# A graph-attention kernel: three late adjacency halves packed and loaded during the plan, two late tiles searched ahead of the first unit

## The reference

```python
h = jnp.maximum(_layernorm(x), 0.0)
hh = jnp.einsum('ni,hif->hnf', h, W)
s1 = jnp.einsum('hnf,hf->hn', hh, a1)
s2 = jnp.einsum('hnf,hf->hn', hh, a2)
scores = leaky_relu(s1[:, :, None] + s2[:, None, :], 0.2)
scores = where(adj[None] > 0, scores, -9e15)
att = softmax(scores, axis=-1)
o = jnp.einsum('hnm,hmf->hnf', att, hh)      # heads side by side: (6144, 512)
return x + elu(o)
```

## Time and profile before

| | us |
|---|---|
| three runs of the kernel before | 792.19, 793.66, 800.2 |
| median | 793.66 |
| the profiled execution | 800.12 |
| its span, from the first to the last instruction | 798.2 |
| VectorE busy in it | 659.8 (83%) |
| TensorE matmuls busy in it | 570.5 (71%) |
| ScalarE, GpSimd busy in it | 469.2, 424.6 |
| granted TensorE clock, mean | 0.848 of full speed |

### The profile page before, as it was taken

One profiled execution on the slowest core, in us unless ns is written; L12 is line 12 of the kernel. 1 busy time (PEld: TensorE's weight loads), 2 busy tenths in 40 slices (PEclk: granted clock), 3 DMA queues, 4 the chain that ended last, 5 costly groups with the idle time before them and its releaser, 6 DMA issues.

```text
span 798.2 us, 9153 instructions
## 1 busy us (share of the span) xinstructions
PE 570.5 (71%) x2182; PEld 407.3 (51%) x2182; DVE 659.8 (83%) x2066; ACT 469.2 (59%) x695; POOL 424.6 (53%) x804
## 2 busy tenths in 40 slices
PE   0389789898877777653777677677767669988770
PEld 0255445554444444342566465556655558766560
DVE  4659988999886767764879998999979989999871
ACT  0777797799999989324265655666455123333231
POOL 4634444443442432227666466647675776888720
PEclk9989999999998989855879879686887769997895
DMA  9999988899999999418989999999998888999986
GB/s 287 423 365 384 349 330 341 338 378 420 419 422 419 419 419 424 196 40 312 389 325 410 414 402 387 406 395 410 392 405 282 216 239 231 284 279 277 285 236 160
DMA packets 65130, 269.51 MB, mean 338 GB/s; under 512 B 12145, under 2 KB 12145, under 8 KB 52786
## 3 DMA queue, kind: packets, MB, share of 16 engines
q1 hardware_dynamic: 32098, 177.95, 55.5%
q0 software_dynamic: 26368, 78.36, 32.3%
q10 hardware_dynamic: 6608, 12.58, 4.2%
HBM read 243.49 MB, written 25.37 MB: 337 GB/s over the span
## 4 chain that ended last, share of the span: by engine, by line
DVE 20%; PE 16%; issue 10%; ACT 3%; another core or an unknown queue 3%; DMA 1%; POOL 1%; POOLq 0%; DVEq 0%; ACTq 0%
DVE nodes L1122 7%; PE psP L1260 5%; PE psP L1261 4%; DVE places L250 3%; PE psP L1267 3%; PE psP L1268 3%; DVE best L239 2%; ACT packed L229 2%; PE psC L1244 2%; DMA nodes<-table,list_column 1%; DVE agg L1134 1%; POOL nodes L959 1%; DVE to_row L1092 1%; DVE result L1142 1%
## 5 line engine op out<-in xcount | busy, mean ns | idle before, releaser
L651 PE MATMUL psH<-sb_W,normedT 128*128 128x512 f32 x384 | 222.5, 671 | 0.0
L229 ACT ACTIVATE packed<-adj_rows,eight 128x3072 uint8<-128x3072 int32 x66 | 188.5, 2856 | 3.8 <-DMA adj_rows<-in_adj_dram 3.2
L954 POOL DMA_INDIRECT nodes<-table,column x138 | 138.5, 1003 | 68.4 <-issue 39.5
L1260 PE MATMUL psP<-nodes,ident 128*128 128x256 f32 x276 | 107.8, 480 | 53.0 <-issue 40.1
L959 POOL DMA_INDIRECT nodes<-table,list_column x109 | 110.8, 1017 | 64.2 <-DVE list_column L1081 33.6
L1122 DVE TENSOR_TENSOR nodes<-nodes,psW 128x2048 f32<-128x2048 f32 (+4 forms) x66 | 138.7, 2142 | 5.1 <-ACT psW L1029 5.0
L698 POOL TENSOR_TENSOR sb_node_sum<-sb_node_sum,h_rows 128x512 f32<-128x512 f32 x48 | 61.1, 1273 | 141.4 <-ACT h_rows L616 141.4
L652 PEld LDWEIGHTS psS<-sb_Wa,normedT 128*128 128x128 f32 x384 | 78.1, 203 | 101.8 <-issue 101.8
L250 DVE FIND_INDEX8 places<-best,packed 128x8 uint32<-128x96 f32 (+6 forms) x240 | 110.4, 468 | 0.0
L239 DVE MAX8 best<-packed 128x8 f32<-128x96 f32 (+6 forms) x240 | 103.2, 463 | 4.5 <-ACT packed L229 4.5
L1261 PE MATMUL psP<-nodes,ident 128*128 128x264 f32 x276 | 104.5, 467 | 0.0
(11 more groups left out here) (177 smaller groups left out, 925.0 us busy)
## 6 DMA issues: line engine op xcount, KB each, us to landing
adj_rows<-in_adj_dram SPq DMA_DIRECT2D x66, 1536.0 KB
sb_adj_rows<-in_adj_dram SPq DMA_DIRECT2D x30, 1536.0 KB, 12.7
table<-h_rows SPq DMA_DIRECT2D x48, 260.0 KB, 8.7
sb_x_rows<-in_x_dram SPq DMA_DIRECT2D x48, 256.0 KB, 8.9
result<-in_x_dram POOLq DMA_DIRECT2D x19, 512.0 KB
out_dram<-result ACTq DMA_DIRECT2D x19, 512.0 KB
result<-in_x_dram POOLq DMA_DIRECT2D x10, 256.0 KB
out_dram<-result ACTq DMA_DIRECT2D x10, 256.0 KB
```

The lines of the kernel that those rows point to most:

```text
L229: nc.scalar.activation(words.bitcast(mybir.dt.uint8), sb["adj_rows"][buffer_of(i)][:], ACT.Square, bias=sb["eight"][:], scale=-17.0, accum ...
L651: nc.tensor.matmul(psH[:, t % 2], normedT[:, t % 2, kc], sb["W"][:, kc], start=(kc == 0), stop=(kc == KC - 1))
L954: nc.gpsimd.indirect_dma_start(out=nodes[:, node_at[u] + i * w.direct + j], out_offset=None, in_=table, in_offset=bass.IndirectOffsetOnAxi ...
L1260: nc.tensor.matmul(low, sb["ident"][:], nodes[:, n, 0:LOW], start=a, stop=False)
```

## The change

The late halves 60, 61 and 62 (both halves of tile 30 and the first of tile 31) are packed by ScalarE in the plan, and the halves 63, 64 and 65 are issued by SyncE in the plan, each behind one of these packs and all ahead of the store of `mean_row` in SyncE's program. In the edges, VectorE searches tiles 30 and 31 ahead of unit 0, in two pieces: the first three MAX8 of tile 30 between `own(1)` and `front(0)`, the rest behind `turn(1)`. Behind units 0 and 6 nothing is searched. Tiles 32 to 36 are searched behind units 1 to 5 (before: 2 to 6), tiles 37 to 47 behind units 7 to 17 as before. The packs follow: half 63 ahead of unit 0, tile 32 in unit 0 to tile 36 in unit 4, none in unit 5, tile 37 in unit 6 and so on as before. The amount of work is the same.

```diff
+GAP = 3
@@ plan
+        @block.scalar
+        def _(act):
+
+            for i in range(2 * EARLY, 2 * EARLY + GAP):
+                pack(nc, act, sb, i // 2, i % 2)
@@
         @block.sync
         def _(sp):
+            for i in range(2 * EARLY + 3, 2 * EARLY + 3 + GAP):
+                load_adj(sp, sb, adj, i)
             sp.wait_ge(mean_ready, 1)
             sp.dma_start(table[N:N + 2].rearrange("(o r) d -> o r d", o=1), mean_row[:]).then_inc(stored, 16)
@@ attend_edges
-    dve_items = [(t, n) for t in range(EARLY, TILES) for n in range(2 * len(segments_of(t)))]
-    dve_round = spread_over([scan_cost(*item) for item in dve_items], COUNTED)
-    rounds_of = {t: [r for (s, _), r in zip(dve_items, dve_round) if s == t] for t in range(EARLY, TILES)}
-    scanned_in = {t: r[-1] for t, r in rounds_of.items()}
-    act_items = [(t, half) for t in range(EARLY, TILES) for half in range(2)]
-    act_round = [rounds_of[t][0] - 1 for t, half in act_items]
+    first_items = [(t, n) for t in range(EARLY, EARLY + 2) for n in range(2 * len(segments_of(t)))]
+    dve_items = [(t, n) for t in range(EARLY + 2, TILES) for n in range(2 * len(segments_of(t)))]
+
+    searchers = [u for u in range(COUNTED) if u not in (0, 6)]
+    dve_round = [searchers[t - EARLY - 2] for t, _ in dve_items]
+    rounds_of = {t: [r for (s, _), r in zip(dve_items, dve_round) if s == t] for t in range(EARLY + 2, TILES)}
+    act_items = [(i // 2, i % 2) for i in range(2 * EARLY + GAP, 2 * TILES)]
+    act_round = [rounds_of[t][0] - 1 if t in rounds_of else -1 for t, half in act_items]
@@ SyncE, edges
-                for i in range(2 * EARLY + 3, 2 * TILES):
-                    if max(0, act_round[i - 3 - 2 * EARLY]) == u:
+                for i in range(2 * EARLY + 3 + GAP, 2 * TILES):
+                    if max(0, act_round[act_items.index(((i - 3) // 2, (i - 3) % 2))]) == u:
                         load_adj(sp, sb, adj, i)
@@ VectorE, edges
             own(0)
             own(1)
+            for t, n in first_items[:3]:
+                scan_step(nc, dve, sb, t, n, EARLY)
             front(0)
             turn(0)
             own(2)
             front(1)
             turn(1)
+            for t, n in first_items[3:]:
+                scan_step(nc, dve, sb, t, n, EARLY)
```

More of the change, by code:

```diff
@@ L709, in _, with plan @@
             add_up(TILES - 1)
-def plan(nc, sb, table):
+def plan(nc, sb, adj, table):
     E, kinds = EARLY_VISITS, EARLY_KINDS
@@ L1534, in build @@
                 project_and_scan(nc, sb, x, adj, table)
-                plan(nc, sb, table)
+                plan(nc, sb, adj, table)
             attend_edges(nc, sb, x, adj, table, out)
```

## The result

| | us |
|---|---|
| the changed kernel, four runs | 801.47, 802.24, 804.83, 807.6 |
| its median | 803.54 |
| the kernel before, beside it, median of four | 794.9 |
| ratio | 1.010, 95% interval 1.0056 to 1.0144 |
| the profiled execution of the changed kernel | 801.47, span 799.8 |

The change makes the kernel slower by 1.0%. A later series of six runs gave 1.0109 (1.0046 to 1.0171). Forecast was 0.4% faster, with a range up to 799.

A forecast was written before the change was run, and what follows sets the result against it. The prediction took VectorE to bound the edges, DMA close behind. Its terms, +3 - 2.0 - 3.3 - 1 = -3.3 us, gave about 790.4 from 793.66; the forecast's own range was 783.5 to 796, the overall one 782 to 799.

The forecast's parts named there:

- The three packs: In the plan, ScalarE has no work, so three packs of about 3.05 us fit, delaying SyncE by about 0.1 us.
- The plan grew: At the plan's end, the `mean_row` store lands behind three loads: 5 us later, between 0.5 and about 8.
- Unit 0: Without its search VectorE saves 4.1 us but waits 2.1 for ScalarE at `weigh(1)`: gain -2.0 us.
- Unit 6: Without its search VectorE saves 5.1 us but waits from 465.8 to about 467.6 for the exponential: gain -3.3 us.
- the start of unit 0: First scores of the edges come 3 us later, from -1.5 to +5.5; fewer contending loads give back 1 to 3.
- They cost nothing themselves: Ahead of unit 0, the searches moved there fit into VectorE's idle time of 13.4 us in all.
- the -1 for remote waits: In the edges, waits the profile calls remote may fall anywhere, from -6.4 to +6 us; -1 was taken.
- What is gained at unit 7 passes to the end: Late in the edges, the gain reaches the kernel's end because VectorE stays busy 47 of 50 us until 750.
- the loads in the loop: In the edges, three fewer loads, 4.7 MB or 11.8 us, keep DMA from becoming the bound but give nothing themselves.
- the third rival: DMA bounds the loop, which gains 11.8 us less the plan's 5: 786.9 us, 0.9% faster; chance 0.10.
- The rival of a remote wait: In unit 0, a remote wait of 12.3 us falls where nothing covers it: 800 us, 0.8% slower; chance 0.18.
- The first rival: In the plan, the store slips through without waiting for the loads: 785 us, 1.1% faster; chance 0.20.

The follow-up runs named there:

- from another queue: Changed kernel with the store of `mean_row` issued by ScalarE behind its packs, the loads staying first on SyncE's queue: 796.09 us, ratio 0.9994.
- half loads: Late loads from half 66 on cut to their first 1536 columns, once in each kernel: changed 783.34 us, ratio 0.9862; before 784.45 us, 0.9890.
- the plan's half: Changed kernel's packs and loads in the plan kept, but nothing searched ahead of unit 0, tile 30 behind unit 0 and so on: 799.74 us, ratio 1.0035.
- one tile ahead: Changed kernel, but only tile 30 searched ahead of unit 0 and tiles 31 to 47 behind units 1 to 17: 798.85 us, ratio 1.0028.
- the second profile of before: The kernel before, unchanged, profiled again in an execution without the 12.3 us remote wait of ScalarE: 794.8 us, one run.
- store first: Changed kernel with one edit: SyncE issues the store of `mean_row` ahead of the three loads in the plan: 792.73 us, ratio 0.9936.
- gap at 13, store last: Changed kernel with one edit: the later unit without a search is 13, not 6; store still behind the loads: 799.51 us, ratio 1.0002.
- the changed kernel's second profile: The changed kernel, unedited, run again with more runs in a later series: 807.42 us, ratio 1.0109.

## Why the prediction was wrong

**What held.** The three packs cost nothing where they were put, in 335.6 to 344.7. The plan grew by 6.5 us; forecast was 5, by the bytes queued ahead of the store. The Trainium skill's ring order (DMA: Bandwidth & Descriptors, queues, rings and completion order) agrees with three positions of one store: 7.7 us to the next block behind the loads, 4.4 from another queue, 2.1 ahead of them. Unit 0: 4.1 us less of search, and 1.89 of waiting for ScalarE (forecast 2.1). Unit 6: 5.1 less, and 1.59 (forecast 1.8). With half loads, where VectorE has hardly a wait for gathers behind unit 0, the terms can be read one by one. The changed kernel begins unit 0 4.0 us later than the one before (38.7 against 34.7; forecast 3) and unit 2 1.8 later, so unit 0 gave 2.2; it begins unit 6 2.0 us later and unit 8 1.3 earlier, so unit 6 gave 3.3. 1.4 us of it are there at unit 14, nothing is left at the end, and the medians are 1.1 apart.

**A term that was mis-sized** is the start of unit 0: +3 forecast, +6.0 measured (41.0 against 35.0). "They cost nothing themselves" is wrong of the searches: in the kernel with only the plan's half, with the same block, unit 0 begins at 36.7, and in the changed one VectorE is busy until 38.8 and then waits for the last gather. That gather took longer, too: the pack of half 63 ahead of unit 0 sends out a load just behind it, which the kernels without a pack there don't have. The changed kernel, then the one with one tile ahead:

```profile
368.21 8.29 DMA nodes<-table,list_column
368.28 0.35 SPq L218 DMA_DIRECT2D adj_rows<-in_adj_dram  x1
```

```profile
367.82 4.37 DMA nodes<-table,list_column
```

The forecast gave back 1 to 3 us for one load in place of two; in the second profile of before, with two loads, the same gather took 8.61. The load alone was not varied, so its part is not shown apart from the rest. Two smaller points of the working: the ends of its own range, 783.5 and 796, are not the sums of its terms' ends, which are 781.9 and 796.9; and the -1 for remote waits has nothing to answer to, since neither the changed kernel's profile nor the second of before has such a wait.

**The step that failed** is "What is gained at unit 7 passes to the end", with the one it leans on, the loads in the loop, of which the text says that three fewer keep "DMA from becoming the bound" and give nothing of themselves. The gain at unit 6 came: the changed kernel is 6.0 us behind the second profile of before at unit 6 and 2.5 behind at unit 8. It did not pass on: 4.1 behind at unit 13, 6.0 at unit 14, 7.5 at the end. DMA was the bound already, at unit 14. Bytes moved since the plan's start, from windows (GB/s times length), in MB:

| | at 17.3 us | 60 | 115 | 145 | 230 | unit 14 at | MB by then |
|---|---|---|---|---|---|---|---|
| before, second profile | 0.5 | 14.4 | 37.0 | 49.2 | 83.1 | 226.4 | 81.7 |
| changed | 4.7 | 15.0 | 37.4 | 46.9 | 80.9 | 232.4 | 81.8 |
| store first | 2.5 | 18.2 | 39.8 | 50.4 | 84.1 | 223.9 | 81.9 |
| gap at 13, store last | 4.7 | 14.7 | 35.1 | 47.4 | 80.0 | 229.0 | 79.7 |

The last column is what ties bytes to time: three kernels that wait 7 to 9 us for unit 14's gathers start it when the same 81.7 to 81.9 MB have been moved (the changed kernel's second profile, with a wait of 5.7 us: 81.1).

The changed kernel leads by the three loads, 4.2 MB, when its plan ends; at 60 us 0.6 MB of that is left. By the program the lead can't grow: there are three buffers, all full, and the next load waits for the next pack; and the gathers begin later by the plan's 6.5 us. Then come units 5 and 6 with two loads in place of four, and GpSimd's gathers don't fill the room: in the two windows here loads moved 4.2 MB against 6.4, and gathers 5.2 against 5.5. The windows, of 30 us each, changed and before (second profile):

```profile
450.55:480.55 30.00, 25.16 (x106) 20.83 (x104) 27.64 (x76) 16.27 (x22) 15.58 (x16) 0.88 0.93 316
```

```profile
451.54:481.54 30.00, 22.32 (x86) 18.34 (x86) 29.45 (x73) 17.66 (x22) 16.76 (x18) 0.83 1.03 406
```

90 GB/s less for 30 us is 2.7 MB. The lead of 0.4 MB at 115 us taken off, 2.3 are missing at 145, and from there to unit 14 both kernels move at the same rate (398 and 399 GB/s), at which 2.3 MB take 5.8 us. That is nearly all of the 6.0 us at unit 14. With the gap at 13 unit 14 begins at 229.0 without a wait and with 79.7 MB moved: the two loads that are left out there are out of the way of its gathers.

So the third rival, DMA as the bound, named the right resource and took the wrong sum. It counted 11.8 us for three loads out of the loop, as if all DMA time were alike, and took off 5 us for the plan. What counts is how much DMA has moved by the time the kernel wants unit 14, and from the plan's start to there the bytes are the same in both kernels: the three loads are moved, not removed. The waits that spoke against that rival, 3.2 us of ScalarE and one of VectorE, came from an execution that was 6.4 us behind the second profile at unit 13 and so was not early enough to wait at unit 14. The rival of a remote wait is open as a cause of the scatter. Three of the thirteen profiles with whole loads show one of over 12 us (of the kernel before, the changed one and one with the gap at 13), and ten do not, with the same load on DMA, so such waits don't "come in every stretch where the DMA engines are full". It is no cause of the change's 1%: the two kernels that are 1.1% apart in one series both have it in their profiles, and the changed kernel's first profile has none.

The first rival (the store slips through) was false as a forecast: the plan's end moved by 6.5 us. What it promised was got by issuing the store first: 1.010 to 0.9936. How the two causes share the loss is open: moving the gap gave 1.1% with the store last, and nothing that can be measured with the store first.

## What to carry to other kernels

A resource whose busy share stands at 1.0 and for which almost nobody waits in one profile is not known to be second; look at a second execution, or halve its bytes, before counting a gain on the engine that seems to lead. When work is moved to an earlier idle stretch, draw the bytes (or the busy time) of the shared resource as a running sum up to the point where it is wanted, for a gap left behind in the middle can cost as much as the hole filled in front brings. And what a block's end waits for is issued ahead of the prefetches, not behind them.

## What the runs showed that was not expected

- Gathers' landing time in 500 to 570 us is 22.0 us in the median with whole loads and 5.3 with half of their bytes.
- After the store of the same two rows of 2080 bytes the next block began in 1.6 us alone, 4.4 us beside loads of another queue, and 7.7 us behind three loads of the same queue.
- The DMA busy share alone doesn't tell the bound: from 500 to 550 us the changed kernel has 1.03 with whole loads (399 GB/s) and 0.95 with half of their bytes (312 GB/s), and in the second no engine waits for DMA there.
- Two executions of one kernel that are 6.4 us apart at unit 13 are 0.6 us apart at unit 14, and the first profile alone had led to the opposite reading.
